# Attention probabilities turned by DMA instead of by TensorE, values computed per block of 128 queries

## The reference, cut to what matters

```python
xn = layernorm(x)                                   # x: 4 x 2048 x 2048
q, k, v = split(xn @ w_atten.T)                     # 16 heads of 128; q, k get rotary positions
att = softmax(where(causal, q @ k.T / sqrt(128), -inf))
s = (att @ v) @ w_proj.T
g = silu(sparsify_2to4(silu(xn @ w_gate) * (xn @ w_up)) @ w_down)   # inner size 8192
out = x + s * g
```

## Time and profile before

| | us |
|---|---|
| median of 3 runs | 2355.92 |
| the profiled execution | 2359.06 |
| its span, first to last instruction, on core 6 (the slowest) | 2357.5 |
| spans of the 8 cores | 2340.6 to 2357.5 |
| mean granted TensorE clock of core 6 | 0.989 |

### The profile page before, as it was taken

How to read it: one execution, slowest core, us unless ns; L and a number is a source line. 1 busy time by engine, 2 the same in 40 slices (tenths; PEclk the granted TensorE clock), 3 DMA queues, 4 the chain that set the end, 5 groups by cost and what they waited for, 6 DMA issues and landing times.

```text
span 2357.5 us, 35698 instructions; the slowest of 8 cores (2340.6 to 2357.5 us)
## 1 busy us (share of the span) xinstructions
PE 2244.5 (95%) x12736; PEld 1189.3 (50%) x12736; DVE 1006.0 (43%) x1441; ACT 617.6 (26%) x1066; POOL 137.0 (6%) x260
## 2 busy tenths in 40 slices
PE   2679999999999998999999999999999999999999
PEld 2546675766757654444444444444444444444444
DVE  4637777676776765003333334444333330100011
ACT  2323344343443334212222222222222210000000
POOL 0000000000000000000000000000000000000000
PEclk9799999999999999999999999999999999999999
DMA  7532213222131323663344344444554569766661
GB/s 218 150 51 54 55 28 71 37 56 55 28 71 37 56 48 65 137 149 72 72 82 80 72 73 85 76 99 90 104 102 90 97 143 251 162 130 129 130 136 47
DMA packets 82732, 217.38 MB, mean 92 GB/s; under 512 B 9984, under 2 KB 30592, under 8 KB 80000
## 3 DMA queue, kind: packets, MB, share of 16 engines
q0 software_dynamic: 36864, 134.23, 34.5%
q1 hardware_dynamic: 44576, 79.94, 10.6%
q10 hardware_dynamic: 1120, 0.92, 0.1%
HBM read 311.53 MB, written 25.17 MB: 143 GB/s over the span
## 4 chain that ended last, share of the span: by engine, by line
PE 77%; DVE 8%; DMA 6%; issue 6%; ACT 1%; DVEq 1%; SPq 0%; ACTq 0%
PE ps L553 36%; PE ps L572 19%; PE ps L431 8%; PE ps L538 5%; DMA arena<-arena 5%; PE ps L442 4%; DVE arena L785 3%; DVE arena L715 2%; PE ps L519 1%; DMA arena<-xN 1%; PE ps L466 1%; PE ps L490 1%; DVE arena L713 1%; PE ps L420 1%; DVE arena L751 1%
## 5 line engine op out<-in xcount | busy, mean ns | idle before, releaser
L553 PE MATMUL ps<-arena 128*128 128x512 bf16 x3968 | 856.6, 379 | 0.0
L553 PEld LDWEIGHTS ps<-arena 128*128 128x128 bf16 x3968 | 388.2, 98 | 468.2
L572 PE MATMUL ps<-arena 128*128 128x512 bf16 x2048 | 442.2, 379 | 1.1 <-DVE arena L836 1.1
L442 PE MATMUL ps<-arena 128*128 128x512 bf16 x1536 | 361.4, 383 | 3.1 <-ACT arena L629 3.1
L836 DVE TENSOR_TENSOR arena<-arena,ps 128x512 f32<-128x512 f32 x124 | 85.0, 686 | 634.0 <-PE ps L553 634.0
L572 PEld LDWEIGHTS ps<-arena 128*128 128x128 bf16 x2048 | 200.3, 98 | 242.9 <-issue 1.5
L431 PE MATMUL ps<-arena 128*128 128x256 bf16 x2048 | 247.4, 277 | 0.0
L442 PEld LDWEIGHTS ps<-arena 128*128 128x128 bf16 x1536 | 146.3, 99 | 154.9 <-issue 10.7
L660 ACT ACTIVATE arena<-ps,arena 128x256 f32<-128x256 f32 (+7 forms) x128 | 156.3, 1221 | 238.8 <-DVE arena L789 238.7
L683 ACT ACTIVATE arena<-arena 128x512 f32<-128x512 f32 x128 | 80.6, 629 | 518.6 <-DVE arena L836 518.6
L431 PEld LDWEIGHTS ps<-arena 128*128 128x128 bf16 x2048 | 200.6, 100 | 26.3
(11 more groups left out here) (51 smaller groups left out, 1378.3 us busy)
## 6 DMA issues: line engine op xcount, KB each, us to landing
arena<-wgu POOLq DMA_DIRECT2D x128, 512.0 KB, 6.4
arena<-wd POOLq DMA_DIRECT2D x64, 512.0 KB, 6.7
arena<-wqkv POOLq DMA_DIRECT2D x48, 512.0 KB, 6.2
arena<-xN SPq DMA_DIRECT2D x16, 1024.0 KB, 6.9
arena<-arena SPq DMA_DIRECT2D x178, 64.0 KB, 2.6
arena<-wp POOLq DMA_DIRECT2D x16, 512.0 KB, 6.2
d_s<-arena SPq DMA_DIRECT2D x32, 256.0 KB, 4.1
d_hT<-arena SPq DMA_DIRECT2D x16, 512.0 KB, 7.0
```

The lines of the kernel that those rows point to most:

```text
L442: mm = e.matmul(bank[:], w[:, f, :], xnv[tile // 2][:, f, (tile % 2) * 512:(tile % 2 + 1) * 512], start=(f == 0), stop=(f == NF - 1))
L553: mm = e.matmul(ps[2 * p + up][:], w[:, f, :], xnv[0][:, f, half * 512:(half + 1) * 512], start=(f == 0), stop=(f == NF - 1))
L572: mm = e.matmul(ps[2 * (fc % 4) + half][:], w[:, j, :], hT[16 * q + j][:, half * 512:(half + 1) * 512], start=(q == 0 and j == 0), stop=(q ...
```

## The change

The exponential is written as bf16 into one of two `pexp` buffers and is not divided by its sum. A DMA transpose on the SP queue turns it, all 128(2j+2) columns in one instruction, into one of three `pT` buffers. `values` runs for each block by itself, two windows later, with the turned block as the stationary operand and 128 columns of values moving; its result has queries on the partitions. ScalarE divides it by the sum while it copies it out (a scale per partition), in bf16, and a second DMA transpose on the SP queue (128x128) puts it into the projection's layout. The 128x128 turning on TensorE, the multiplication by the reciprocal and the copies of turned blocks are gone. The bank that the turning used goes to the units, which now rotate over three. The swaps of rotary positions are issued by ScalarE behind its own copy. STEPS is changed: 14, 14, 20, 21, 22, 22, 23, 24 in the first 14 heads (before 17, 18, 19, 20, 20, 21, 22, 23; the sum is 160 in both), 113 and 95 steps in the last two heads (before 104 and 104).

```diff
-STEPS = [17, 18, 19, 20, 20, 21, 22, 23] * (2 * NG - 2)
-STEPS += [12, 13, 13, 14, 14, 14, 12, 12, 12, 12, 12, 13, 13, 13, 14, 15]
+STEPS = [14, 14, 20, 21, 22, 22, 23, 24] * (2 * NG - 2)
+STEPS += [7, 8, 14, 15, 17, 19, 16, 17, 7, 8, 11, 13, 13, 14, 14, 15]
...
-    pexp = A.alloc(8 * KB)
-    pbf = A.alloc(4 * KB, BF16)
-    pT = A.alloc(8 * KB, BF16)
+    pexp = [A.alloc(4 * KB, BF16) for _ in range(2)]
+    pT = [A.alloc(4 * KB, BF16) for _ in range(3)]
...
+        def turn_p(w):
+
+            e.wait_ge(S["a_ex"], w + 1)
+            if w >= 3:
+                e.wait_ge(S["p_pv"], w - 2)
+            n = 2 * (w % NB + 1)
+            e.dma_start_transpose(out=pTv[w % 3][:, 0:n, :], in_=pexp[w % 2][:, 0:128 * n]).then_inc(S[f"dT{w % 2}"], 16)
+
+        def turn_y(w):
+
+            h, j = w // NB, w % NB
+            e.wait_ge(S["a_y"], w + 1)
+            e.dma_start_transpose(out=yav[:, h:h + 1, j * 128:(j + 1) * 128], in_=y_sb[w % 2][:]).then_inc(S[f"dY{w % 2}"], 16)
...
+        for w in range(NW + 2):
+            if w >= 2:
+                turn_y(w - 2)
+            if w < NW:
+                turn_p(w)
...
-                bank = ps[4 + u % 2]
-                if s0 == 0 and u >= 2:
-                    e.wait_ge(S["a_u"], u - 1)
+                bank = ps[4 + u % 3]
+                if s0 == 0 and u >= 3:
+                    e.wait_ge(S["a_u"], u - 2)
...
+        def values(w):
+
+            h, n = w // NB, 2 * (w % NB + 1)
+            e.wait_ge(S[f"dT{w % 2}"], 16 * (w // 2 + 1))
...
+            for k in range(n):
+                mm = e.matmul(ps[7][:, 0:128], pTv[w % 3][:, k, :],
+                              v[:, k * 256 + (h % 2) * 128:k * 256 + (h % 2 + 1) * 128],
+                              start=(k == 0), stop=(k == n - 1))
...
-            if pv is not None:
-                values(pv)
             steps(parts[0])
-            if w:
-                turn_p(w - 1)
+            if w >= 2:
+                values(w - 2)
             steps(parts[1])
...
+            e.activation(y_sb[w % 2][:], ps[7][:, 0:128], AF.Copy, scale=rc[w % 3][:, 0:1]).then_inc(S["a_y"])
...
+                if w >= 2:
+                    e.wait_ge(S[f"dT{w % 2}"], 16 * (w // 2))
...
+                e.activation(pexp[w % 2][:, 0:ncol], psum[:, 0:ncol], AF.Exp, bias=nm[w % 2][:], scale=SCALE,
+                             accum_out=den[w % 3][:]).then_inc(S["a_ex"])
+            for u in ended(parts[0]):
+                leave(u)
+            if w >= 2:
+                leave_y(w - 2)
+            for u in ended(parts[1]):
+                leave(u)
...
-                e.tensor_scalar_mul(pbf[:, 0:ncol], pexp[:, 0:ncol], rc[b][:, 0:1]).then_inc(S["v_nr"])
```

More of the change, by code:

```diff
@@ L152, in window_table @@
     pos = 0
[L153 to L161, removed]
+    for w in range(NW):
+        a = STEPS[w] // 2
+        rows.append((cut(pos, pos + a), cut(pos + a, pos + STEPS[w])))
+        pos += STEPS[w]
     assert pos == 16 * (len(UNITS) - NSTART)
-    return rows
+    return rows + 2 * [([], [])]
 WINDOWS = window_table()
@@ L185 @@
 LN_UNITS, LN_ROPES = ln_tables()
-LEAVE_EARLY = [ended(WINDOWS[w][1][0]) for w in range(NW + 1)]
-LEAVE_LATE = [ended(WINDOWS[w][1][1]) for w in range(NW + 1)]
+LEAVE = [ended(a) + ended(b) for a, b in WINDOWS]
 def build_nc():
@@ L221, in build_nc @@
     nm = [A.alloc(1) for _ in range(2)]
-    den = [A.alloc(1) for _ in range(2)]
-    rc = [A.alloc(1) for _ in range(2)]
+    den = [A.alloc(1) for _ in range(3)]
+    rc = [A.alloc(1) for _ in range(3)]
+    y_sb = [A.alloc(64, BF16) for _ in range(2)]
     assert A.ptr <= KB
@@ L243, in build_nc @@
     PEXP = A.ptr
-    pexp = A.alloc(8 * KB)
-    pbf = A.alloc(4 * KB, BF16)
-    pT = A.alloc(8 * KB, BF16)
-    pTv = pT[:].rearrange("p (k x) -> p k x", x=256)
+    pexp = [A.alloc(4 * KB, BF16) for _ in range(2)]
+    pT = [A.alloc(4 * KB, BF16) for _ in range(3)]
+    pTv = [v[:].rearrange("p (k x) -> p k x", x=128) for v in pT]
     ROPE = A.ptr
@@ L457, in turn_x @@
                 mm.then_inc(S["p_xt"])
-        def turn_p(w):
-            n = 2 * (w % NB + 1)
-            e.wait_ge(S["v_nr"], w + 1)
+        def values(w):
+            h, n = w // NB, 2 * (w % NB + 1)
+            e.wait_ge(S[f"dT{w % 2}"], 16 * (w // 2 + 1))
+            e.wait_ge(S["a_u"], max(u for u, un in enumerate(UNITS) if un[:2] == (h // 2, "v")) + 1)
             if w:
[L464 to L485, removed]
-            v = vg[(h // 2) % 2]
[L487 to L491, removed]
+                e.wait_ge(S["a_y"], w)
+            v = vg[(h // 2) % 2]
+            for k in range(n):
+                mm = e.matmul(ps[7][:, 0:128], pTv[w % 3][:, k, :],
+                              v[:, k * 256 + (h % 2) * 128:k * 256 + (h % 2 + 1) * 128],
+                              start=(k == 0), stop=(k == n - 1))
             mm.then_inc(S["p_pv"])
@@ L505, in prog_tensor @@
         e.wait_ge(S["dMK"], 16)
-        for w, (pv, parts) in enumerate(WINDOWS):
+        for w, parts in enumerate(WINDOWS):
             if w < NW:
@@ L587, in leave @@
                     e.wait_ge(S["p_s"], 8 * (H - 1))
-                e.copy((graw if kind == "gate" else uraw)[g][:], ps[4 + u % 2][:]).then_inc(S["a_u"])
+                e.copy((graw if kind == "gate" else uraw)[g][:], ps[4 + u % 3][:]).then_inc(S["a_u"])
             elif kind == "v":
@@ L647, in prog_scalar @@
             u += 1
-        for w, (pv, parts) in enumerate(WINDOWS):
-            if pv is not None:
-                leave_y(pv)
-            for u in LEAVE_EARLY[w]:
-                leave(u)
+        for w, parts in enumerate(WINDOWS):
             if w < NW:
@@ L790, in prog_vector @@
             if w:
-                leave_p(w - 1)
-                for u in LEAVE_EARLY[w - 1] + LEAVE_LATE[w - 1]:
+                b = (w - 1) % 3
+                e.wait_ge(S["a_ex"], w)
+                if w >= 4:
+                    e.wait_ge(S["a_y"], w - 3)
+                e.reciprocal(rc[b][:], den[b][:]).then_inc(S["v_rc"])
+                for u in LEAVE[w - 1]:
                     if u in ROPE_NO:
```

81 lines of the change are left out of this document (19 added, 62 removed).

## The result

The change made the kernel 0.7% slower: the ratio of the runs is 1.0071, 95% interval 1.0040 to 1.0102. That is clear of noise, but inside the 2% that the prediction counts as no change. The profiled execution took 2374.36 us (span 2372.7 on core 2) against 2359.06. I had forecast 2288. The attention stage, forecast at 717.5 us, takes 801.6.

What follows compares the result with a forecast made beforehand. TensorE's work was taken as the bound: heads of 43.3 + 0.5 + 1.1 us, with first head, last two and tail, gave a 717.5 us stage against 785.9, so 2288 us (own range 2262 to 2313; 8 in 10: 2262 to 2490).

Steps and rivals of the forecast that it cites:

- What bounds the kernel, and TensorE's work: Attention stage: bound thinly by TensorE's work, 47.2 of 49.4 us per head, falling to 43.3 with the change.
- Turning by DMA: Widest block's turning, taken to land in 5.5 us: TensorE waits 1.1 us per head, 3.3 in heads 14 and 15.
- X: Time from issue to landing of the widest block's turning (512 KB): 5.5 us taken, between 2.4 and 7.0.
- Swaps and ropes: ScalarE's swap issue and ropes ahead of a maximum delay exponentials: 0.5 us per head, between 0 and 1.5.
- Tail: From the last scores to the projection: 16.8 us, against 15.7 before.
- Queue-bound: Rival: SyncE's queue turns piece by piece at 0.53 us each; stage 782 us, time 2352 us; chance 0.23.
- Turning-bound: Rival: turning itself slower, from 0.61 us per piece on; at 0.70, 2486 us; at the skill's figure, above 3200; chance 0.27.
- The chain of exponentials: Rival: swaps and late ropes cost 1.5 us per head, stage 14 us longer, 2302 us; inside the forecast's range.

Runs made afterwards that it cites:

- e17: e12 with the swaps of rotary positions left out from the ninth on, weight loads still running: 2287.34 us (one run).
- e18: e9 also without the swaps from the ninth on, leaving turnings and a few loads; read on core 7: span 2291.5 us, stage 721.5.
- e8: Kernel before with one part of the change alone, the swaps issued by ScalarE instead of SyncE: ratio 1.0010.
- e12: Changed kernel, weight loads held until given values are done, the last until the last y is turned; block turned ahead of y on SyncE's queue: ratio 0.9936.
- e2: Kernel before without the 42 q, k, v weight loads of head pairs 1 to 7 (pair 0's weights used): 2351.26 us, one run.
- e1: Changed kernel without the 42 q, k, v weight loads of head pairs 1 to 7 (pair 0's weights used): 2325.31 us, one run.
- e9: e1 with all but three of the output projection's weight pieces held until the last y is turned: 2317.61 us, one run.
- e4: Changed kernel with a window's two turnings exchanged on SyncE's queue, the block ahead of the y: ratio 1.0081.

## Why the prediction was wrong

*What bounds the kernel, and TensorE's work:* right. Without the swaps, heads 2 to 13 take 43.5 us on the mean (e17, median of the cores) against 43.3 of work. That the stage of e17 on its slowest core (714.8) and its head 14 (38.4) come out at my 717.5 and 38.4 is luck: e17 has no swap and turns the block first, and by my own terms with a landing of 4.3 us that is 14 x 43.3 + 2 + 35.1 + 28.4 + 15.6 for the tail + 1 of waits = 688. The 26 us above it are the first two heads (11), one window behind two loads in head 15 (9) and small excesses elsewhere; the median of the cores, 702.3, is 14 above.

*Turning by DMA, the step that failed:* "I take 5.5 ... as nothing here crosses to memory". As a size X was even too large: the widest block lands after 4.3 us with nothing beside it (e18) and 4.5 in the odd heads of after. It failed as a constant. X is the landing in company, and the weight loads and swaps cross the same 16 engines: 7.9 us beside two loads, and 24.5 for 10 pieces beside a pile. I had priced each transfer on its own row and never put the POOL queue's loads beside the turnings, though two loads go out together at the end of every second head, just ahead of the widest turning. So the wait of values came out at 67.9 us, where my sum had 14 x 1.1 + 2 x 3.3 = 22.

*Swaps and ropes, "0.5 us per head":* moving the issue to ScalarE cost nothing in the kernel before (e8), but the term counted only ScalarE's time. That landings grow beside turnings I had written under what would show me wrong, with no price. VectorE waits for them 49.3 us in before, 95.3 in after and 127.7 in e12. Loads and turnings each add to it: 8.2 us with neither (e2), 38.7 with the turnings alone (e1), 49.3 with the loads alone (before). The lateness beside loads was thus in the kernel before too, and cost its stage little (the 6 us of e2).

*Where the 84 us of the stage are:* the fourteen heads take 693.9 against 630.6 (+63), head 14 48.9 against 38.4 (+10.5), the last with the tail 58.8 against 48.5 (+10). By the experiments, as medians of the cores' stages (788.7 in after; e18 of one die), the loads of `wqkv` are 44 of it (e1: 744.2), the late `wp` loads 10 (e9: 734.7), the swaps beside turnings 14 (e18: 720.7). On the slowest cores the same steps are 51, 6 and 23. Each of these runs is one execution, and the parts depend on each other: with the loads held but running and the order exchanged, taking the swaps out gave 58 us on the slowest cores, 65 by the medians (e12 to e17). Whether the loads or the order make the difference is not shown. A part of the loss is the clock behind the waits: over the span 0.979 was granted on the mean, against 0.989 before.

*Tail:* 16.8 forecast, 18.4 measured from last scores to projection; the turning of y and the last block queue behind each other.

*Rivals.* Queue-bound: its time was nearest, its reason false, as a quiet 16-piece turning holds the queue for 1.9 us in e18 and 2.3 in after, 0.12 to 0.14 a piece and not 0.53. Turning-bound: false for the same reason; e17 keeps every turning and has none of its times. The Trainium skill (VectorE: DVE Perf Modes, The three transpose paths) gives 1309 ns for a piece by DMA; here sixteen pieces land after 4.3 to 4.5 us, under 0.3 each, so its figure doesn't hold for pieces in one instruction. The chain of exponentials: right in that the wait reappears there (e4, e12), by the ropes that stand ahead of the maximum; its 14 us were too few.

*Not settled:* how much of the swap's price is its slower issue on ScalarE and how much its late landing; both went in e17. And the long windows in the last heads of e18, and the price of the old STEPS.

## What to carry to other kernels

When work moves to a DMA, its landing in quiet is a lower bound: list everything that crosses the DMA engines in the same windows, by queue, and see who waits behind each of them, small transfers included. A mean DMA share doesn't show it (0.67 in e17 from 255 to 776 us with TensorE idle for under 1 us, 0.60 in after with 92 us of waits); the bursts do (0.90 from 354 to 368 us in after). Then time the background loads by the progress of the consumer, which here turned +0.7% into −0.9%, and look next at small latency-bound DMAs, such as the swaps: avoiding them or moving them away from the turnings was not tried here in a kernel that does all the work.
